# Attention and MoE dispatch on one core: GpSimd adds two chunks of probabilities, TensorE's row sums go from four parts to three, router steps move up

## The reference

```
x = x + xcond(layernorm(x), ctx, ctx, k_length)
    s    = SCALE * log(k_length)[:, None, None, None]
    attn = softmax(s * einsum('bhdq,bhdk->bhqk', qh, kh), axis=-1)
    out  = einsum('bhqk,bhdk->bhdq', attn, vh)
x = x + ffn(layernorm(x), Wg, w1, w2)
    probs = softmax(xr @ Wg);  gate_vals, expert_idx = top_k(probs, 2)
    # each expert takes its first C = 1280 rows in order; then
    h = relu(dispatched @ w1);  expert_out = h @ w2;  out = sum of gate * expert_out
```

## Time and profile before

| | us |
|---|---|
| median of 3 runs | 2199.55 (2198.3 to 2199.72) |
| the profiled execution's own time | 2198.8 |
| its span in the profile | 2197.1 |
| TensorE busy | 2117.3 (96%) |
| VectorE busy | 1017.1 (46%) |
| ScalarE busy | 713.2 (32%) |
| GpSimd busy | 476.6 (22%) |

### The profile page before, as it was taken

One profiled execution on the slowest core, in us unless ns is written; L12 is line 12 of the kernel. 1 busy time (PEld: TensorE's weight loads), 2 busy tenths in 40 slices (PEclk: granted clock), 3 DMA queues, 4 the chain that ended last, 5 costly groups with the idle time before them and its releaser, 6 DMA issues. The chain is left out here.

```text
span 2197.1 us, 26958 instructions
## 1 busy us (share of the span) xinstructions
PE 2117.3 (96%) x10098; PEld 1509.5 (69%) x10098; DVE 1017.1 (46%) x1903; ACT 713.2 (32%) x1214; POOL 476.6 (22%) x598
## 2 busy tenths in 40 slices
PE   4999999999995999999999999999999999999997
PEld 2444454444445888878888888887888788888776
DVE  5777888878854434224423423332432342343211
ACT  1666666666652222112212212211321221131110
POOL 3334444343422210210301111031030102101101
PEclk9999999999996999999999999999999999999999
DMA  9877777777725344222613522522351252342101
GB/s 147 161 164 148 180 158 186 164 175 165 153 96 153 107 92 125 51 40 79 136 20 71 128 53 40 126 66 40 99 113 21 60 125 47 59 116 39 14 9 19
DMA packets 184460, 216.70 MB, mean 99 GB/s; under 512 B 40295, under 2 KB 111983, under 8 KB 184304
## 3 DMA queue, kind: packets, MB, share of 16 engines
q1 hardware_dynamic: 154692, 173.28, 34.3%
q0 software_dynamic: 22240, 37.92, 8.9%
q10 hardware_dynamic: 7372, 3.42, 0.7%
HBM read 113.93 MB, written 68.29 MB: 83 GB/s over the span
## 5 line engine op out<-in xcount | busy, mean ns | idle before, releaser
L1251 DVE SCALAR_TENSOR_TENSOR hlo<-ps_h,hhi 128x512 fp32r<-128x512 f32 x256 | 177.0, 692 | 934.4 <-ACT hhi L1129 934.4
L1129 ACT ACTIVATE hhi<-ps_h 128x512 fp32r<-128x512 f32 x256 | 152.8, 597 | 1128.5 <-PE ps_h L1392 1128.5
L1411 PE MATMUL ps_y<-w2hi,hlo 128*128 128x512 f32 x1024 | 404.5, 395 | 1.8 <-issue 1.8
L1390 PE MATMUL ps_h<-xhi,w1hi 128*128 128x512 f32 x1024 | 404.5, 395 | 1.3 <-PEq L976 1.3
L1409 PE MATMUL ps_y<-w2hi,hhi 128*128 128x512 f32 x1024 | 404.3, 395 | 0.7 <-DVE hlo L1251 0.7
L1391 PE MATMUL ps_h<-xlo,w1hi 128*128 128x512 f32 x1024 | 404.8, 395 | 0.0
L1410 PE MATMUL ps_y<-w2lo,hhi 128*128 128x512 f32 x1024 | 404.6, 395 | 0.0
L1392 PE MATMUL ps_h<-xhi,w1lo 128*128 128x512 f32 x1024 | 404.4, 395 | 0.0
L564 DVE TENSOR_REDUCE nmax<-ps_s 128x1 f32<-128x512 f32 x512 | 335.5, 681 | 122.3 <-PE ps_s L773 118.4
L430 ACT ACTIVATE probs<-ps_t 128x512 f32<-128x512 f32 x512 | 278.5, 603 | 193.6 <-PE ps_t L783 153.5
L1390 PEld LDWEIGHTS ps_h<-xhi,w1hi 128*128 128x128 f32 x1024 | 192.3, 188 | 49.0 <-issue 2.6
(11 more groups left out here) (158 smaller groups left out, 1998.1 us busy)
## 6 DMA issues: line engine op xcount, KB each, us to landing
raw<-in_L_ffn_w SPq DMA_DIRECT2D x128, 512.0 KB, 4.8
qst<-qhi SPq DMA_DIRECT2D x64, 256.0 KB, 5.8
xin<-dispatched SPq DMA_DIRECT2D x60, 256.0 KB, 5.8
kst<-khi SPq DMA_DIRECT2D x52, 256.0 KB, 6.2
xt<-in_x SPq DMA_DIRECT2D x32, 256.0 KB, 3.0
ct<-in_ctx SPq DMA_DIRECT2D x32, 256.0 KB, 4.3
qst<-qlo SPq DMA_DIRECT2D x32, 256.0 KB, 7.1
xres<-in_x SPq DMA_DIRECT2D x32, 256.0 KB, 4.3
```

The lines of the kernel that those rows point to most:

```text
L1129: nc.scalar.activation(hhi[k % 2][:], ps_h[k % 3][:], ACT.Relu).then_inc(hhi_ready, 1)
L1251: nc.vector.scalar_tensor_tensor(hlo[k % 2][:], ps_h[k % 3][:], 0.0, hhi[k % 2][:].bitcast(F32), ALU.max, ALU.subtract).then_inc(h_ready, 1)
L1390: nc.tensor.matmul(to, w1hi[:, c, fs], xhi[n % 2][:, c, :], start=(c == 0), stop=False)
L1411: done = nc.tensor.matmul(ps_y[b][:], hlo[k % 2][:, bs], w2hi[:, f, :], start=False, stop=(f == NF - 1))
```

## The change

Four things are done together.

GpSimd adds the probabilities of key chunks 0 and 1 of a group into a new buffer, `pair_sum`, in four operations of 128x512 (`sum_pairs`, one per head). They stand in its queue behind the residual and ahead of `qlo`. The row sums on TensorE then take three parts, `pair_sum`, chunk 2 and chunk 3, in place of four.

The visits are three in place of four: none behind chunk 1; behind chunk 2 two `ps_o` sections (chunks 0 and 1); behind chunk 3 one `ps_o` section and the `ps_l` section of `pair_sum`; behind the next step's chunk 0 one `ps_o` section and two `ps_l` sections. Chunk 3's exponentials go into the buffer of chunk 0, so ScalarE now waits for GpSimd's addition of the same head ahead of each.

On VectorE, in odd steps, the router's operations stand a turn to three turns earlier. On GpSimd the dispatch stands first in the step in place of behind the residual.

`spare_over` now lies in the memory of `x2t`, to make room.

```diff
+            def sum_pairs(g):
+                if g >= 1:
+                    pool.wait_ge(pv_done, 3 * (g - 1) + 2)
+                for i in range(HPG):
+                    pool.wait_ge(t_free, t_turn["t", g, 1, i])
+                    nc.gpsimd.tensor_tensor(pair_sum[:, i, :], probs[(4 * g) % 3][:, i, :], probs[(4 * g + 1) % 3][:, i, :],
+                                            ALU.add).then_inc(pairs_summed, 1)
+
             for s in range(-2, SLOTS):
+                if pair_in(s - 1):
+                    dispatch((s - 8) // 2)
...
                 if live(s - 4) and not late(s):
                     residual(s - 4)
-                if pair_in(s - 1):
-                    dispatch((s - 8) // 2)
+                if live(s - 2):
+                    sum_pairs(s - 2)
...
-                            if i == 0 and n >= 3:
-
-                                act.wait_ge(pv_done, n - 2)
+                            g = s - 2
+                            if c == 3:
+                                act.wait_ge(pairs_summed, HPG * g + i + 1)
+                                if i == 0:
+                                    act.wait_ge(pv_done, 3 * g + 1)
+                            elif i == 0 and g >= 1:
+                                if c == 0:
+                                    act.wait_ge(pairs_summed, HPG * g)
+                                    act.wait_ge(pv_done, 3 * g - 2)
+                                else:
+                                    act.wait_ge(pv_done, 3 * g)
...
-                        if (c, i) == (1, 0) and pair_in(s):
+                        if (c, i) == (0, 3) and pair_in(s):
                             n = (s - 7) // 2 + 1
                             dve.wait_ge(rt["lexp"], 2 * n)
...
-                        if (c, i) == (1, 3) and pair_in(s):
+                        if (c, i) == (1, 1) and pair_in(s):
                             n = (s - 7) // 2 + 1
                             dve.wait_ge(rt["topi"], n * 2)
...
-                        if (c, i) == (2, 1) and pair_in(s):
+                        if (c, i) == (1, 2) and pair_in(s):
...
+            def summed(g, c):
+                if c == 1:
+                    pe.wait_ge(pairs_summed, HPG * (g + 1))
+                    if g >= 1:
                         pe.wait_ge(l_saved, g)
                 for h in range(HPG):
                     hd = slice(HD * h, HD * h + HD)
-                    nc.tensor.matmul(ps_o[hd, :], vt[g % 4][:, c, hd], probs[n % 3][:, h, :],
-                                     start=(c == 0), stop=(c == NC4 - 1))
-                for h in range(HPG):
-                    hd = slice(HD * h, HD * h + HD)
-                    done = nc.tensor.matmul(ps_l[hd, :], ones[:, 0:HD], probs[n % 3][:, h, :],
-                                            start=(c == 0), stop=(c == NC4 - 1))
-                done.then_inc(pv_done, 1)
+                    done = nc.tensor.matmul(ps_l[hd, :], ones[:, 0:HD], (pair_sum if c == 1 else probs[(4 * g + c) % 3])[:, h, :],
+                                            start=(c == 1), stop=(c == NC4 - 1))
+                return done
...
                     if c == 0 and live(s - 3):
-                        weighted(s - 3, NC4 - 1)
-                    if c > 0 and live(s - 2):
-                        weighted(s - 2, c - 1)
+                        weighted(s - 3, 3)
+                        summed(s - 3, 2)
+                        summed(s - 3, 3).then_inc(pv_done, 1)
+                    if c == 2 and live(s - 2):
+                        weighted(s - 2, 0)
+                        weighted(s - 2, 1).then_inc(pv_done, 1)
+                    if c == 3 and live(s - 2):
+                        weighted(s - 2, 2)
+                        summed(s - 2, 1).then_inc(pv_done, 1)
```

More of the change, by code:

```diff
@@ L153, in attention_and_dispatch @@
         x2t = sb("x2t", [P, D])
+        spare_over = x2t[:, 0:E * FILLS].rearrange("p (e n) -> p e n", e=E)
         lg = [sb(f"lg{i}", [P, 2, E]) for i in range(2)]
@@ L465, in _ @@
                         g = s - 3
[L466 removed]
+                        act.wait_ge(pv_done, 3 * (g + 1))
                         if g >= 2:
@@ L623, in _ @@
                             nc.vector.reciprocal(zinv[:], zsum[:]).then_inc(rt["zinv"], 1)
-                        if (c, i) == (1, 1) and pair_in(s):
+                        if (c, i) == (1, 0) and pair_in(s):
                             n = (s - 7) // 2 + 1
@@ L649, in _ @@
                                                     ALU.subtract).then_inc(r_ready, 1)
-                        if (c, i) == (1, 2) and pair_in(s):
+                        if (c, i) == (1, 1) and pair_in(s):
                             n = (s - 7) // 2 + 1
@@ L752, in weighted @@
                         pe.wait_ge(o_saved, g)
+                pe.wait_ge(t_free, t_turn["t", g, c, HPG - 1])
+                for h in range(HPG):
+                    hd = slice(HD * h, HD * h + HD)
+                    done = nc.tensor.matmul(ps_o[hd, :], vt[g % 4][:, c, hd], probs[(4 * g + c) % 3][:, h, :],
+                                            start=(c == 0), stop=(c == NC4 - 1))
+                return done
[3 more added lines that the diff above has]
+                    if g >= 1:
                         pe.wait_ge(l_saved, g)
```

15 lines of the change are left out of this document (6 added, 9 removed).

## The result

The changed kernel takes 2277.68 us in the median of 4 runs (2274.43 to 2280.17), the kernel before 2199.64 beside it. The ratio is 1.0354, with a 95% interval of 1.0337 to 1.0372. The forecast was 2208 us with a range of 2180 to 2231: the sign was right, the size was far off. The profiled execution took 2277.95 us, its span is 2276.2.

The account below looks back on a forecast made before the run. TensorE was taken as the bound, VectorE 0.5 and 0.1 us behind. +11 us over 27 full steps, -2 at the start and 0 for the drain gave +9 on 2198.8: 2208 us, range 2180 to 2231.

Parts of the forecast that it names:

- The holds: VectorE's cast, subtraction and `qf` in chunk 2 stand still until GpSimd's running operation ends; one slips through per boundary.
- H: Delay of `qf`'s end at (2, 3) by these holds: 2.2 us in odd steps, 2.5 or 1.3 in even.
- The place of the last waiting product: TensorE's (3, 3) starts 3.17 us + H + 0.1 after the cast's start, 12.3 (odd) or 11.0 (even) into the step.
- the step ends 2.41 later: From TensorE's (3, 3) to the odd step's end takes 2.41 us as before, giving a step of 20.2 against 19.55.
- The sum: 27 full steps give +11 us, the three starting steps -2, the drain 0: +9 us, 2208 us in all.
- The signs that were named: Subtraction and `qf` near 1.1 us, cast 0.17 to 1.2, VectorE near 90, TensorE waits some 2 us a step.
- The ceiling of 37 us: On TensorE, one section and one visit less saves 1.15 us a step, over 32 groups at most 37 us.
- A: VectorE is not in the way and TensorE's gain comes through: -0.5 even, -0.85 odd, 2178 us; chance 0.16.
- B: VectorE's held operations catch GpSimd's boundaries, the delay near 1.4 us in both steps: 2189 us; chance 0.20.
- C: Gain and holds even out, with the delay near 1.7 us: 2196 to 2203 us; chance 0.16.
- D: Router's two counts at (1, 2) are held too, another 1.1 us in odd steps: 2231 us; chance 0.13.
- E: ScalarE's chunk 3 exponentials wait for GpSimd's additions, 1.2 us each; costs only as in A, no chance of its own.

Follow-up runs that it names:

- e4: Changed kernel plus four extra TensorE products of 512 columns per step in chunk 3, their result overwritten: 2241.50 us, 1.0181 of the kernel before.
- e8: e7 plus the four extra TensorE products per step in chunk 3 whose result is overwritten: 2223.28 us, 1.0078 of the kernel before.
- e1: Changed kernel without GpSimd's four additions per step, so row sums lack chunks 0 and 1: 2203.42 us, 1.0008 of the kernel before.
- e5: Kernel before with only the router's VectorE operations and GpSimd's dispatch moved up as in the change: 2192.82 us, 0.9959 of the kernel before.
- e7: Changed kernel with the cast and subtraction of `r_hl` moved to GpSimd and `qf` moved from (2, 3) to (3, 2): 2197.08 us, 0.9970 of before.
- e9: e7 with GpSimd splitting `r_hl` behind its fourth addition, not its first, in the two drain steps: 2188.82 us, 0.9960 of the kernel before.
- e10: e9 with chunk 0's output products back in a visit of their own behind chunk 1, making four visits: 2185.57 us, 0.9946 of before.
- e2: Kernel before plus four GpSimd additions of constants per step, behind the residual and ahead of the dispatch, result unused: 2252.9 us, 1.0233 of before.
- e6: e5 plus four GpSimd additions of constants per step at the changed kernel's place, visits as before: 2247.43 us, 1.0181 of the kernel before.
- e3: Changed kernel with chunk 0's output products back in a visit of their own behind chunk 1, making four visits: 2295.58 us, 1.0427 of before.

## Why the prediction was wrong, point by point

*The reading of before* held. VectorE stands right behind TensorE, and a hold of VectorE becomes a wait of TensorE.

*The holds.* Forecast was that one VectorE operation slips through at each boundary, with H = 2.2 us in odd and 2.5 or 1.3 us in even steps. Measured is 2.1 in the mean. In the even step shown it is 1.9 (0.48 + 1.21 + 1.13, less the 0.88 that the three take alone), in the odd one 2.5 (1.09 + 1.21 + 1.11, less 0.88). The sum took 2.2 for odd steps and, as the middle of 2.5 and 1.3, 1.9 for even ones: 0.3 short in the one, right in the other. In the even step the cast caught a boundary, though not for the reason given (it came later, see below). `hot` and `picked` came free (0.19 and 0.18), as forecast.

*The place of the last waiting product* came near in the odd step and not in the even one. The odd step's first turns run partly at 1.2 GHz, which costs some 0.3 us up to its first section (287.18, 2.40 us in place of the 2.08 of the earlier trace rows), the even one's cost 0.7 (307.80 to 310.60 is 2.80). Less these, the products at 303.07 and 325.55 are 18.0 and 17.0 us into their steps. The forecast was 18.0 + 2.2 - 2.41 = 17.8, and 16.8 + 1.9 - 2.53 = 16.2. The even step's 0.8 us are a smaller miss of its own: the cast was to start at 11.0 and starts at 12.5, which is 11.8 less the 0.7. The transposes were to come 1.15 us earlier; the second four come 0.4 earlier (318.45, 9.9 us into the step less the 0.7), and 0.37 us of the rest is a wait of TensorE for ScalarE's exponentials just ahead of them.

*The step that failed* is the one that followed: "the step ends 2.41 later", and the 2.53 of the even step. These are times of a TensorE at 2.4 GHz, carried over into a step in which it isn't. Behind the waits the clock falls, and the same stretch of work takes 4.73 and 4.05 us; the first products of the next step are slow as well. Over the steady part a pair of steps is 44.3 us (23.4 and 20.9 from transpose to transpose), where 38.9 was forecast (20.2, and 18.7 as the middle of the even step's outcomes). The clock is 5.0 of the missing 5.4: it is 0.887 in the mean of 200 to 500 us (0.90, 0.86 and 0.90), and 0.113 of 44.3 is 5.0. e4 shows it by a run: the same holds, half the time at 1.2 GHz, 36 us less; and e8, where the same filler costs time, shows that the gain is not the filler's own.

*The sum.* Without the clock it would have been fair: +9 us was forecast for attention, +15.9 is what the table leaves at full clock, which is arithmetic, since no run had these holds with the clock up. The clock is a term of +67 us that the sum did not have. No rival had it either: all of them move only what is held and who waits, with TensorE at 2.4 GHz throughout, so the range could not reach it.

*The signs that were named* to watch: the means came as said (1.215, 1.123 and 0.659 us), VectorE's share did not go near 90 but down to 78.23, since the step grew by more than its work, and the steps were 2.8 and 3.1 us longer than forecast. TensorE's waits for VectorE's reductions were to be some 2 us a step; they are 12.0 us in 300, 0.9 a step. So the waits were smaller than forecast and the loss was larger: it can't be the waits alone.

*The ceiling of 37 us* for the sections removed was too high. With the additions free of charge 16.5 us of it come through (e1 less e5). In e1 TensorE has new waits in place of the work: 4.6 us for `o_sb`, 3.0 for ScalarE's exponentials and 2.0 for reductions in 300 us, 0.6 a step. VectorE and ScalarE are too close behind to let TensorE run ahead.

*The rivals.* A, that VectorE is not in the way, had 2178 us: when its three operations are taken out of the way (e7, e9, e10), 2186 to 2197 is what comes of it. (The -0.85 us that A took for odd steps has no working behind it.) B and C had H at 1.4 and 1.7; it is 2.1. D, the counts held too, did not happen (0.16 and 0.17 us), but by luck: `klo` starts at 339.16, 0.12 us behind the start of the second count at 339.04, and so in all seven odd steps of 200 to 500 us. In e2, where the counts stand later, they were held by 1.5 us. E was right in its condition: in the changed kernel ScalarE waits for an addition 3 times in 300 us, but in e7, where VectorE no longer comes first, 28 times, for 15.0 us in all:

```profile
ACT probs L462 <- POOL pair_sum L361: 15.0, 28, 1.0
```

The Trainium skill (TensorE: Matmul & The Clock Gate, "HAM oscillation — how this bites in real kernels") describes a loop in which a wait in every iteration brings the clock down in every iteration, and prices it at half of the time spent at the low level. These traces agree, although TensorE is busy for 93.19 of 100 us and its waits are under a microsecond each: half of the time at 1.2 GHz is 66.9 us in the changed kernel and 31.7 in e4, and of the difference of 35.2 us the run gained 34.7. The page was not weighed in the prediction, where it would have made a rival.

The Trainium skill (SBUF — State Buffer, "Who interferes with whom") says that whoever issues first blocks the other, so that GpSimd suffers as well. The sum left this out with an estimate of 0.6 us a step. The trace agrees with the rule: an addition takes 1.364 us beside the three VectorE operations and 1.273 in e7, where two of them are gone, 0.36 us over four, with `qf` still beside them. So the term was real, and about what was estimated or less.

*What stays open.* Why one row of short waits brings the clock down and another doesn't was not tried: in e7 TensorE is busy for 9.15 of 10 us from 296 to 306, and its clock stays at 1.00, while at the same place of other steps it falls three times:

```profile
296.00:306.00 10.00, 9.15 (x51) 4.55 (x44) 7.46 (x27) 7.25 (x13) 5.61 (x9) 1.00 0.54 81
```

And e2 spreads its loss otherwise than e6 (19.2 and 31.7 us of clock); the holds are not the same in the two, but why the clock falls less in e2 was not followed up. Which of the three held operations costs the most is open as well.

## What to carry to other kernels

TensorE was busy for 99 of 100 us here, and the new waits in each step had two prices: the waits themselves (16 us, less what was saved), and what TensorE loses at 1.2 GHz behind them (67 us). Make the second a rival of its own whenever a change puts waits into each step of a loop. Before handing work to GpSimd, look at which small VectorE operations (casts, scalings, two-input operations from SBUF) will stand beside the new row: it was 2 us a step for three of them, and moving two to GpSimd and the third three turns on took 80 us off the kernel. All that the additions then bring over the router's moves alone is 2 to 5 us, no more than the noise. A busy time that grows while work was removed is a sign to read the clock row first.

## What the runs showed of the hardware that was not expected

- In the changed kernel TensorE's granted clock fell to the 1.2 GHz level at the end of every step shown, behind windows of 2 us in which it was idle for 0.4 to 0.8 us, and stayed there for 3.4 or 6.8 us, though its mean busy share was 93 in 100. In e7 it stayed at 1.00 over 10 us with 0.85 us idle.
- Four products a step that do nothing made a kernel 36 us faster (e4), and made another one 26 us slower (e8).
- A cast and a subtraction of 64x32 took 0.20 and 0.25 us on GpSimd (e7) and 0.66 and 1.22 on VectorE beside GpSimd's row (after); alone they take 0.17 and 0.18 on VectorE. The engine that is slightly slower for them was the faster place.
- A visit more cost 10.4 us at full clock where VectorE was held (e3 against after) and nothing where two of the three held operations had left VectorE (e10 against e9), although the third, `qf`, was held for 1.0 us in e10.
